# Token maximum of y: one VectorE reduction over 2048 values in place of two over 1024 and a join

## The reference, cut to what matters

```python
gate = bitlinear(x, w_gate)                  # 2048 features per token
up = bitlinear(x, w_up)
intermediate = jax.nn.silu(gate) * up
return h_bitlinear(intermediate, w_down)     # einsum(act_quant(fwht(x)), weight_quant(w))

def act_quant(x, bits=ACT_BITS):
    qb = float(2 ** (bits - 1))
    scale = qb / jnp.clip(jnp.max(jnp.abs(x), axis=-1, keepdims=True), EPS)
    xq = jnp.clip(jnp.round(x * scale), -qb, qb - 1) / scale
```

## Time and profile before

| | us |
|---|---|
| median of 3 runs (419.92 to 420.31) | 420.11 |
| the profiled execution, its own time | 419.76 |
| its span, first to last instruction | 417.8 |
| PE busy | 388.4 (93% of the span) |
| DVE busy | 365.6 (88%) |
| ACT busy | 291.3 (70%) |
| POOL busy | 175.3 (42%) |
| mean granted TensorE clock | 0.995 of full speed |

### The profile page before, as it was taken

How to read it: one execution, slowest core, us unless ns; L and a number is a source line. 1 busy time by engine, 2 the same in 40 slices (tenths; PEclk the granted TensorE clock), 3 DMA queues, 4 the chain that set the end, 5 groups by cost and what they waited for, 6 DMA issues and landing times.

```text
span 417.8 us, 7359 instructions
## 1 busy us (share of the span) xinstructions
PE 388.4 (93%) x2170; PEld 270.2 (65%) x2203; DVE 365.6 (88%) x653; ACT 291.3 (70%) x450; POOL 175.3 (42%) x207
## 2 busy tenths in 40 slices
PE   1899999999999989989999999999999999999891
PEld 1347788888887564756666666666666666667740
DVE  6788587779888889999999999999999999998970
ACT  4446686587875243658888888888888888877960
POOL 0667310114124111053575575575575575522021
PEclk9999999999999999999999999999999999999997
DMA  7759474065000000235155155155155155255241
GB/s 244 268 160 417 154 247 157 1 211 192 2 15 0 13 14 8 57 63 103 44 109 126 44 107 126 44 107 126 43 107 126 43 107 126 48 106 113 50 102 50
DMA packets 48969, 43.66 MB, mean 105 GB/s; under 512 B 42673, under 2 KB 42801, under 8 KB 46897
## 3 DMA queue, kind: packets, MB, share of 16 engines
q1 hardware_dynamic: 44224, 27.11, 22.6%
q0 software_dynamic: 4720, 16.26, 16.5%
HBM read 21.33 MB, written 4.19 MB: 61 GB/s over the span
## 4 chain that ended last, share of the span: by engine, by line
PE 78%; DVE 11%; issue 5%; DMA 3%; ACT 2%; POOL 1%; DVEq 0%; SPq 0%; POOLq 0%; ACTq 0%
PE bank L465 21%; PE bank L588 13%; PE bank L595 11%; PE bank L564 10%; PE bank L571 10%; PE bank L427 9%; DVE prod L1182 2%; DVE ct_lo L972 1%; DMA xs<-x_dram,order 1%; PE bank L532 1%; DMA yqT<-yq 1%; PE bank L681 1%; DVE bfly L1209 1%; DVE mixed L1209 1%; DVE xs L1100 1%
## 5 line engine op out<-in xcount | busy, mean ns | idle before, releaser
L588 PEld LDWEIGHTS bank<-cst,mT 128*128 128x128 f32 x512 | 66.5, 191 | 12.9 <-issue 2.1
L588 PE MATMUL bank<-cst,mT 128*128 128x128 f32 x512 | 67.7, 276 | 3.4 <-ACT mT L836 3.4
L571 PE MATMUL bank<-wq,xqT 128*128 128x512 bf16 x232 | 61.0, 379 | 0.4
L595 PE MATMUL bank<-wq,yqT 128*128 128x512 bf16 x227 | 59.3, 379 | 1.6 <-DMA yqT<-yq 0.8
L564 PE MATMUL bank<-wq,xqT 128*128 128x512 bf16 x231 | 59.8, 379 | 0.5
L836 ACT ACTIVATE mT<-bank 128x512 f32<-128x512 f32 x64 | 37.6, 592 | 17.9 <-PE bank L427 17.9
L410 POOL DMA_INDIRECT out_dram<-res,order x16 | 19.4, 1215 | 70.4 <-DVE res L1309 70.4
L824 ACT ACTIVATE y<-y,yqs 128x512 int8<-128x512 f32 x56 | 40.2, 718 | 11.8 <-POOL yqs L368 11.8
L841 ACT ACTIVATE y<-bank 128x512 f32<-128x512 f32 x64 | 37.6, 588 | 9.7 <-PE bank L588 9.5
L861 ACT ACTIVATE sg<-bank,gate_s 128x512 f32<-128x512 f32 x60 | 41.0, 683 | 4.1 <-PE bank L564 3.9
L1182 DVE TENSOR_TENSOR prod<-bank,sg 128x512 f32<-128x512 f32 x64 | 43.3, 677 | 0.6 <-ACT sg L861 0.5
(11 more groups left out here) (154 smaller groups left out, 806.4 us busy)
## 6 DMA issues: line engine op xcount, KB each, us to landing
mixed<-mixed POOLq DMA_DIRECT2D x15, 512.0 KB, 5.3
stage<-ctx_dram SPq DMA_DIRECT2D x4, 1024.0 KB, 7.7
stage<-wgate_dram SPq DMA_DIRECT2D x4, 1024.0 KB, 8.1
stage<-wup_dram SPq DMA_DIRECT2D x4, 1024.0 KB, 4.7
stage<-wdown_dram SPq DMA_DIRECT2D x4, 1024.0 KB, 4.7
yqT<-yq SPq DMA_TRANSPOSE x60, 2.4
cst<-consts_dram SPq DMA_DIRECT2D x1, 274.0 KB, 2.9
xs<-x_dram,order POOLq DMA_INDIRECT x16, 4.4
```

What stands on the lines that cost most here:

```text
L571: last = nc.tensor.matmul(ps_up[n % 2][:, :], xqT[:, b, c, :], wq[:, 1, c * F + 512 * n:c * F + 512 * (n + 1)], start=(c == 0), stop=(c == ...
L588: last = nc.tensor.matmul(bank_[:, c * P:(c + 1) * P], mT[:, n % 2, c, :], had, start=True, stop=True)
L595: last = nc.tensor.matmul(ps_down[b][:, :], yqT[:, m, g, :], wq[:, 2, block_ * D:(block_ + 1) * D], start=(m == 0 and g == 0), stop=(m == ...
```

## The change

The maximum of tile t-3 is taken in one reduction over all 2048 values, `y_max_whole`, at the head of section n = 0, where the second half stood. The first half in section n = 2 and the join in n = 0 are gone. `y_max_whole` writes `ymax` directly and waits for the same semaphore value as the second half did. In the drain tile 13 is treated likewise, and `end_scales` skips the join where it is given one part; tiles 14 and 15 keep theirs.

```diff
--- before.py
+++ after.py
@@ -1289,6 +1289,12 @@
                                                      AX_X, ALU.max, apply_absolute_value=True))
 
 
+            def y_max_whole(t, b, s):
+
+                dve.wait_ge(y_set, t * NQ + NQ)
+                return s.did(nc.vector.tensor_reduce(ymax[:, b:b + 1], y[:, b, :], AX_X, ALU.max,
+                                                     apply_absolute_value=True))
+
             def y_max_all(b, s, part_step, parts=2):
                 s.wait(part_step)
                 return s.did(nc.vector.tensor_reduce(ymax[:, b:b + 1], ymax_part[:, b, 0:parts], AX_X, ALU.max))
@@ -1319,8 +1325,8 @@
                         ln_quantise(t + 1, o)
                     if isinstance(t, int) and t == 2 and n == 1:
                         ln_quantise(4, 0)
-                    if rnd and n == 0 and gu:
-                        y_step = y_max(t - 3, o, 1, (2, 4), s)
+                    if rnd and n == 0:
+                        y_step = y_max_whole(t - 3, o, s)
                     if bf:
                         if n == 0:
                             dve.wait_ge(prod_set, (t - 1) * NQ + NQ)
@@ -1330,8 +1336,6 @@
                             dve.wait_ge(mT_done, (t - 3) * NQ + NQ)
                         if n < 3:
                             s.did(butterfly(o, n, 0))
-                    if rnd and n == 0 and not gu:
-                        y_step = y_max(t - 3, o, 1, (2, 4), s)
                     if rnd and n == 1:
                         y_reciprocal(t - 3, o)
                     if fin and n == 3:
@@ -1341,14 +1345,10 @@
                             butterfly(o, n, 1).then_inc(mixed_set, 1)
                         else:
                             bfly_step = s.did(butterfly(o, n, 1))
-                    if rnd and n == 0:
-                        y_step = y_max_all(o, s, y_step)
                     if ln and n == 1:
                         max_step = ln_max(t + 1, o, s)
                     if ln2 and n == 3:
                         ln_stats(t + 2, b, s)
-                    if ym and n == 2:
-                        y_max(t - 2, b, 0, (0, 2), s)
                     if gu:
                         multiply(t, b, n)
                     if ln and n == 1:
@@ -1370,7 +1370,8 @@
             def end_scales(t, step, parts):
 
                 b = t % 2
-                step = y_max_all(b, st, step, parts)
+                if parts > 1:
+                    step = y_max_all(b, st, step, parts)
                 y_clip(t, b, st, step)
                 y_reciprocal(t, b)
                 dve.wait_ge(yrec_set, t + 1)
@@ -1383,9 +1384,9 @@
                 c = C % 2
                 dve.wait_ge(prod_set, C * NQ + NQ)
                 st.did(butterfly(c, 0, 0))
-                step = y_max(A, A % 2, 1, (2, 4), st)
+                step = y_max_whole(A, A % 2, st)
                 level = st.did(butterfly(c, 0, 1))
-                end_scales(A, step, 2)
+                end_scales(A, step, 1)
                 for n in (1, 2):
                     st.wait(level)
                     if n == 2:
```

## The result

The changed kernel takes 428.04 us, median of 6 runs (427.14 to 429.25), beside 420.19 for the kernel before in the same session (6 runs, 419.56 to 420.35). The ratio is 1.0191, 95% interval 1.0176 to 1.0205: slower by 7.9 us. The prediction said 427.6 (423.5 to 430.5), slower. The profiled execution took 427.42 us, its span is 425.6.

What follows compares the result with a forecast made beforehand. TensorE was taken as the bound, VectorE nearly full. Losses of 0.80 (t = 3), 6.27 (11 openings at 0.57), 0.50 (t = 15) and 0.3 (drain) sum to 7.9 us on 419.76: 427.6 us, range 423.5 to 430.5.

Steps and rivals of the forecast that it cites:

- Reduction, 2.30 us and 2.21 in the stream: VectorE's opening reduction over 2048 values takes 2.30 us, 2.21 until the next starts; bounds in the stream 1.13 and 2.26.
- VectorE's work, 0.11 less in a step: Half reduction and join removed, opening reduction lengthened: VectorE's work in a step falls by 0.11 us.
- Everything 1.02 late: All behind the opening reduction, from the multiply through `yamax`, `out_s` and `yqs` to ScalarE's copy, comes 1.02 us later.
- TensorE, 0.50 late and 0.08 dearer: TensorE's Hadamard product behind the copy of quarter 2 starts 0.50 us late and takes 0.08 more: 0.58 a step.
- VectorE's path, 0.58: Late `ln_round` delays VectorE's `xq` by 0.66 us, so the next opening is 0.58 later; 0.57 taken for each of 11.
- t = 3, 0.80: At t = 3, where TensorE already waited 1.31 us, 1.02 is paid less 0.22 from an earlier opening: 0.80 us.
- t = 15, 0.50: At t = 15, which has no `ln_round`, the TensorE path alone costs up to 0.50 us; 0.50 taken.
- The drain, 0.3: In the drain the long reduction delays the last tile's `mixed` and TensorE's transposes; 0.3 us gets through.
- (a): Rival: TensorE's room of 0.52 us is absent, each of 13 steps pays the whole 1.02; 433 us, chance 0.08.
- (d): Rival: the reduction over 2048 is as short as a half now, nothing late, TensorE the bound; 419.5 us, chance 0.04.
- (c): Rival: VectorE is the true bound, its 0.11 us less in each of 13 steps comes out; 418.3 us, chance 0.05.
- (b): Rival: part of the lateness is absorbed on GpSimd or ScalarE, 0.25 us in a step; 424 us, chance 0.10.

Runs made afterwards that it cites:

- e1: Kernel before with both half reductions at the head of section n = 0, drain too, join where it was; 431.27 us, ratio 1.0277.
- e5: Changed kernel with `finish` issued ahead of `ln_quantise` on VectorE in section n = 3; 427.44 us, ratio 1.0172.
- e2: Kernel before with the two reductions cut 512 early and 1536 late, places kept; 421.51 us, ratio 1.0050.
- e6: Changed kernel with the clip ahead of the multiply of n = 0 and the reciprocal behind it; 425.68 us, ratio 1.0141.
- e7: Changed kernel with clip and reciprocal one slot earlier and `finish` ahead of `ln_quantise`, whole reduction kept; 419.01 us, ratio 0.9985.
- a2: Changed kernel unaltered, one more profiled execution; 427.27 us.
- e4: Changed kernel, but in n = 1 ScalarE copies the new quarter of y before it waits for `yqs`; 424.22 us, ratio 1.0113.
- e8: e7 with tile 13, whose maximum is taken in the drain, in two halves again; 419.05 us, ratio 1.0004 to e7.
- e3: Changed kernel with clip and reciprocal one slot earlier, the clip between the butterfly halves of n = 0; 421.22 us, ratio 1.0041.

## Why the prediction was right

By its own steps:

- **Reduction, 2.30 us and 2.21 in the stream.** Its line shows 2.25 to 2.29, and 261.28 - 259.11 = 2.17 in the stream. The bound from above, two halves, is e1: 2.24. The bound from below is out.
- **VectorE's work, 0.11 less in a step.** The starts give 1.13 + 1.12 + 0.06 - 2.17 = 0.14 less. None of it is seen in the time, nor in VectorE's busy sum, since waits break up the stream and an operation behind a wait overlaps none before it.
- **Everything 1.02 late.** 0.98, at `yamax`, `yqs`, the copy and `ln_round` alike: 0.04 less for the shorter reduction. `out_s` kept its 2.29 and `ffn_shift` fell to 0.27, as worked out.
- **TensorE, 0.50 late and 0.08 dearer.** In the shown step 0.36 and 0.11; as the sole path (e5) 0.45 in a step, not 0.58. The product started 0.05 after the copy's end, 269.50 - 269.45, not the 0.15 taken from the wait at t = 3. The wait at 588 that was named as a sign is there in all 11 steps, but 0.23 to 0.30 us long, not about half a microsecond.
- **VectorE's path, 0.58.** It governs, by e5. In the shown step the starts on VectorE hold 0.24 us of waiting ahead of the multiply of n = 2, 0.64 ahead of `xq` and 0.06 behind it, 0.94 in all. Of this 0.14 is the saved work. The wait ahead of the multiply, for silu on ScalarE, was not foreseen; the prediction put all of the idle time ahead of `xq`. Before, the opening's room was not the 0.11 of the prediction but 0.19 by the starts (271.25 - 270.99 less the 0.07 that the same two starts are apart now). 0.94 - 0.14 - 0.19 = 0.61 against the step's 16.30 - 15.67 = 0.63. Its neighbour gains 0.46. Predicted 0.57 in each of 11 steps, 6.27; measured 178.28 - 172.40 = 5.88.
- **t = 3, 0.80.** 194.21 - 178.93 = 15.28 against 192.90 - 178.65 = 14.25: 1.03, less the 0.22 to 0.23 by which its own opening came earlier relative to the copy. 0.80, as predicted. All of the lateness is paid where TensorE was waiting before. Its wait grew by more, from 1.31 to 2.82 us, because TensorE also gets there 0.7 earlier: in the kernel before the removed first half at t = 2 had held up `mixed`, for which its transposes waited,
```profile
...
178.27 0.63 PE L427 MATMUL bank<-cst,mixed 128*128 128x128 f32 x4 [0.51 <-DVE mixed L1201]
...
```
  and in the changed kernel they start at 178.10 without a wait, though its copy of y comes 0.50 later.
- **t = 15, 0.50.** From the boundary of the earlier trace rows at 365.30 the kernel before took 16.07 us to the drain's reduction at 381.37; now 389.07 - 372.49 = 16.58: 0.51. In the trace the opening itself stands at 365.26; by it the 11 steps cost 5.92 and t = 15 costs 0.47, the same together.
- **The drain, 0.3.** The last tile's transposes and their copy, TensorE first, then ScalarE:
```profile
...
399.25 1.06 PE L427 MATMUL bank<-cst,mixed 128*128 128x128 f32 x8 [0.56 <-DVE mixed L1201]
...
399.91 1.09 ACT L836 ACTIVATE mT<-bank 128x512 f32<-128x512 f32 x2 [0.23 <-PE bank L427]
...
```
  The copy starts 10.84 behind the drain's opening at 389.07; before 391.88 - 381.37 = 10.51. So 0.33 gets through here, as said, but only 0.1 to the end (36.53 against 36.43).
- **The sum.** 0.80 + 5.88 + 0.51 + 0.10 = 7.3, against 7.9. The remaining 0.4 of the difference between the profiled executions, 427.42 - 419.76 = 7.7, lies ahead of the copy that opens t = 3 (it starts at 178.30, before 177.80), where the change does not reach. This part differs between executions of one kernel too: the changed kernel's t = 3 opens at 178.93, and at 178.62 and 177.89 in two more.

Of the rivals, (a) falls with the steps, which lost 0.54 and not 1.02, and with e2 (there is room of 0.5 us); its 433 also counted t = 3 with 1.02, where the forecast had 0.80. (d) falls with the reduction's 2.25. (c) is out because `out_s` never took the short way, 2283 ns on the mean of 13, and e6 shows what it takes: `out_s` started ahead of the adds. Its idea that VectorE bounds is half true: VectorE's path governs, but by its waits, not by its work. (b) is out: a step lost 0.54, not 0.25. That the forecast and the median agree within 0.5 us is partly luck. The mechanism is worth 7.3, and half of the six runs have 1.5 more, which no step of the prediction named.

## What to carry to other kernels

An operation merged to save VectorE time must be priced by when its last input and its result come, not by its length: here 0.14 us a step was saved and the result came 0.98 later. Somewhat under half of that was free in the full steps, 0.54 was paid in each of 11, and 0.80 at t = 3, where TensorE was already waiting. Before merging, follow the result to the first engine that already waits for it and take the room behind that; then try to use the result earlier (e7). In the late place the merged form was the cheaper one (e1); whether it also beats two halves with an early clip is not shown. Where two paths close within 0.1 us of each other, easing one alone shows little, as in e5.

## What the runs showed of the hardware that was not expected

**TensorE's clock after a long wait.** The profile shows two levels of the clock that TensorE was granted, 1.00 (2.4 GHz) and 0.50 (1.2 GHz). In e5's profiled execution, 429.25 us, TensorE's eight products at 588 behind the wait of t = 3:
```profile
...
188.56 2.05 PE L588 MATMUL bank<-cst,mT 128*128 128x128 f32 x8 [2.81 <-ACT mT L836]
...
```
Windows of e5, columns as in the earlier trace rows; the granted clock is the third number from the end:
```profile
...
186.00:189.00 3.00, 0.44 (x2) 0.47 (x3) 2.60 (x3) 2.91 (x6) 2.66 (x3) 0.80 0.12 29
189.00:192.00 3.00, 3.00 (x14) 2.49 (x14) 2.37 (x3) 2.22 (x6) 0.25 (x1) 0.50 0.26 59
192.00:195.00 3.00, 3.00 (x11) 1.44 (x10) 0.14 (x2) 1.90 (x4) 0.64 (x1) 0.56 0.66 130
195.00:198.00 3.00, 3.00 (x21) 1.96 (x20) 2.34 (x4) 1.48 (x3) 1.00 (x3) 1.00 0.88 94
...
```
The same product in the changed kernel:
```profile
...
189.36 1.13 PE L588 MATMUL bank<-cst,mT 128*128 128x128 f32 x8 [2.82 <-ACT mT L836]
...
```
And the window behind it:
```profile
...
189.40:191.40 2.00, 2.00 (x15) 1.64 (x16) 0.97 (x3) 2.00 (x5) 0.05 (x1) 1.00 0.29 66
...
```
After the same idle time, 2.8 us, the clock was at its lower level, 1.2 GHz, in one execution and at 2.4 GHz in the other. In e5 the step t = 3 took 196.37 - 178.13 = 18.24 us against 15.28, so 3.0 were lost there; e1's trace (eight products in 2.04 after 2.94 idle) and e6's (a granted clock of 0.50 from 189 to 192) show a fall of about half that length. e5's runs stand at 425.6, 427.5 and 429.25 with mean granted clocks of 0.995, 0.991 to 0.992 and 0.987: none, one or two times about 1.8 us. In the changed kernel the upper group had 0.988 to 0.991 and the lower 0.993 to 0.994. Two more executions of it were profiled to see a fall at t = 3:

> The changed kernel unaltered, one more profiled execution. Its executions fell into two groups, 427.1 to 427.5 (mean granted clock 0.993) and 428.6 to 429.3 (0.988 to 0.991). If the 1.5 us between them is the fall of TensorE's granted clock after its long wait at the step t=3 (as the traces of e1, e5 and e6 had it), an execution near 428.9 shows 0.50 in the stretch behind 189.4 us and eight L588 products of about 2.0 us there, and an opening of t=4 about 1.5 us late; one near 427.3 shows 1.00 and 1.15 us. An execution near 428.9 with the clock at 1.00 there refutes it.

> As a2: the changed kernel unaltered, a third profiled execution, so that one of each group may be seen. Near 428.9: granted clock 0.50 behind the wait at t=3 and the opening of t=4 at about 195.7 to 196.4 instead of 194.2; near 427.3: 1.00 and 194.2.

Measured: 427.27 and 426.51 us, both with 2.81 us of idle time, 1.00 behind it, and eight products in 1.13. They are of the lower group and fit, but no trace of the upper group was caught. So of six traces with a wait of 2.67 to 2.94 us at t = 3, three show the fall (e1, e5, e6) and three do not (the changed kernel three times); e4's and e2's, with shorter waits there, 2.33 and 2.2, show none. That the upper group's 1.5 us are this fall is therefore inferred from e1, e5 and e6 and from the mean clocks, not shown. Nor is the wait at t = 3 all of it. Before, it was 1.31 us, and still 1 run of 13, beside e1 to e4, stood at 421.50, and 2 of 22, beside e5 to e8, at 421.01 and 421.14. e8's eight products at t = 3 follow no idle time in its trace, and 3 of its 12 runs are 2 to 4.5 us high. What decides in which runs the clock falls stays open.

**Small GpSimd operations and VectorE's adds.** One started with a pair of adds ends with the pair (2.29, 2.30), also where VectorE's reciprocal stands between the two, as at 265.41 between the adds at 264.27 and 265.48 of the changed kernel; one started with a single add ends with it (1.17 in e3); and beside a long reduction or a multiply with an input in PSUM it takes 0.26 or 0.27. The operation thus ends when the adds end, whichever it is; the three sizes fit a wait and not a slower rate. The Trainium skill (GPSIMD Engine Reference, Specifications) names contention with VectorE's instructions that have two SBUF inputs, and the traces agree; here the operation takes up to nine times its own length.
